# The causal mask of latent attention: a select by index on GpSimd behind the exponential, in place of mask products on TensorE

## The reference

```python
x = x + 0.5 * moe(layernorm(x))            # 8 experts, top 2
x = x + attn(layernorm(x))                 # 16 heads, causal, key offsets by slope
x = x + 0.5 * moe(layernorm(x))
x = x + 0.5 * latent_block(layernorm(x))   # latent attention + small experts
x = x + scan_block(layernorm(x))           # convolution, recurrence, FFN
x = x + 0.5 * latent_block(layernorm(x))
```

```python
att = einsum('bhqd,bhkd->bhqk', q, k) / sqrt(64)
att = where(tril(ones(t, t)), att, -inf)      # key index <= query index
y = einsum('bhqk,bhkd->bhqd', softmax(att), v)
```

## Time and profile before

| | us |
|---|---|
| median of 3 runs | 1462.42 |
| the three runs | 1457.88, 1462.42, 1463.39 |
| the profiled execution | 1457.45 |
| its span, first to last instruction | 1455.6 |
| TensorE busy | 1343.7 |
| VectorE busy | 1006.8 |
| ScalarE busy | 866.9 |
| GpSimd busy | 396.7 |

### The profile page before, as it was taken

The page is one execution under the profiler, slowest core; times in us unless marked ns, Lnnn a source line. Parts: engine busy times, 40 slices in busy tenths (PEclk is TensorE's granted clock), DMA queues, the critical chain, the costliest instruction groups (busy, mean ns, idle before and its releaser), DMA issues.

```text
span 1455.6 us, 27093 instructions
## 1 busy us (share of the span) xinstructions
PE 1343.7 (92%) x10934; PEld 571.7 (39%) x10934; DVE 1006.8 (69%) x1516; ACT 866.9 (60%) x1100; POOL 396.7 (27%) x331
## 2 busy tenths in 40 slices
PE   7899998898889999989999989899988999989997
PEld 5344343333334444433444333443333444433432
DVE  3534778889815457778978757978867687766734
ACT  4344357788773562546567687566765766546672
POOL 5554420011014654522222023021232042202010
PEclk8999999999999999979999999999998999989998
DMA  6623101000005331101111010111010110101100
GB/s 173 118 58 69 33 5 44 3 2 2 2 1 109 121 68 24 26 6 23 34 24 23 1 23 1 34 24 23 1 23 1 23 34 6 26 8 23 24 1 15
DMA packets 30291, 45.80 MB, mean 31 GB/s; under 512 B 5892, under 2 KB 10692, under 8 KB 30116
## 3 DMA queue, kind: packets, MB, share of 16 engines
q1 hardware_dynamic: 30168, 44.08, 13.8%
HBM read 25.39 MB, written 1.18 MB: 18 GB/s over the span
## 4 chain that ended last, share of the span: by engine, by line
PE 76%; ACT 10%; DVE 8%; issue 5%; DMA 0%; POOL 0%; POOLq 0%; ACTq 0%; DVEq 0%; SPq 0%
PE ps L1251 14%; PE ps L1351 12%; PE ps L1296 8%; ACT PR L1429 6%; PE ps L1217 6%; PE ps L1237 5%; PE ps L1218 5%; PE ps L1219 5%; PE ps L1831 3%; DVE BM L1517 2%; PE ps L1315 2%; PE ps L1229 2%; PE ps L1258 2%; PE ps L1362 2%; PE ps L1363 1%
## 5 line engine op out<-in xcount | busy, mean ns | idle before, releaser
L1429 ACT ACTIVATE PR<-ps 128x1024 f32<-128x1024 f32 x432 | 432.4, 1025 | 220.8 <-PE ps L1258 126.2
L1517 DVE TENSOR_REDUCE BM<-ps 128x2 f32<-128x1024 f32 (+2 forms) x384 | 349.6, 951 | 48.0 <-PE ps L1237 47.4
L1251 PE MATMUL ps<-QS,KS 48*128 48x512 f16 (+7 forms) x2688 | 310.5, 333 | 46.6 <-ACT PR L1429 35.0
L1351 PE MATMUL ps<-PR,VS 128*32 128x512 f32 (+3 forms) x2304 | 234.3, 501 | 3.6 <-ACT PR L1429 3.1
L1251 PEld LDWEIGHTS ps<-QS,KS 48*128 48x128 f16 (+1 forms) x2688 | 109.9, 96 | 214.5 <-ACT PR L1429 111.1
L1237 PE MATMUL ps<-KS,QS 48*128 48x128 f16 (+2 forms) x1728 | 161.4, 274 | 15.6 <-DVE BM L1517 6.5
L1510 DVE TENSOR_REDUCE BM<-ps 128x8 f32<-128x1024 f32 x96 | 116.9, 1220 | 35.4 <-PE ps L1237 34.7
L1237 PEld LDWEIGHTS ps<-KS,QS 48*128 48x128 f16 x1728 | 69.0, 95 | 129.2 <-issue 48.0
L1217 PE MATMUL ps<-YA,QS 128*128 128x512 f16 x256 | 99.8, 390 | 1.1 <-DVE RX L1476 1.0
L1558 POOL TENSOR_TENSOR OS<-OS,RX 128x512 f32<-128x512 f32 x24 | 30.5, 1272 | 255.4 <-ACT RX L1445 255.4
L1218 PE MATMUL ps<-YA,QS 128*128 128x512 f16 x256 | 99.3, 388 | 0.0
(11 more groups left out here) (299 smaller groups left out, 2070.3 us busy)
## 6 DMA issues: line engine op xcount, KB each, us to landing
PR<-gates SPq DMA_DIRECT2D x32, 512.0 KB, 11.9
QS<-KS SPq DMA_DIRECT2D x64, 128.0 KB
QS<-KS SPq DMA_DIRECT2D x64, 64.0 KB
WM<-W_in SPq DMA_DIRECT2D x1, 2048.0 KB, 9.1
QS<-HL SPq DMA_DIRECT2D x48, 32.0 KB
KS<-HL SPq DMA_DIRECT2D x48, 32.0 KB
QS<-CT SPq DMA_DIRECT2D x96, 2.0 KB
KS<-KS SPq DMA_DIRECT2D x8, 128.0 KB, 2.4
```

The source lines that it names most:

```text
L1251: ins = pe.matmul(ps[pair][:, w, off:off + cols], KS[rows, ks, kt * P:(kt + 1) * P], QS[rows, qs, (ph + 1) * TT - cols:(ph + 1) * TT], sta ...
L1351: ins = pe.matmul(dst[32 * j:32 * j + 32, TT - cols:TT], v, PR[:, buf, j, off:off + cols], start=(g == 0), stop=(g == NGRP[ph] - 1))
L1429: act.activation(dst, src, ACT.Exp, scale=0.125 if lat else 1.0).then_inc(sig["exp"], 1)
L1517: ins = dve.tensor_reduce(BM[:, ph, p, :, qt - 4 * ph, part], bnk[:, :, off:off + nk * P], AX.X, ALU.max)
```

## The change

For the latent layers alone, the four mask products of each diagonal piece are not issued. The exponential is taken of the unmasked scores. A new GpSimd task `mk` follows the last exponential of each masked group: for every diagonal square of the group one `affine_select` over four heads by 128 queries, in place in `PR`, keeps the element where query index minus key index is not negative and writes 0 elsewhere. `pv` of such a group waits for `mk` in place of the exponential. In the planner the new task costs 0.66 us a square and stands second in GpSimd's order of preference; the masked score steps of the latent plan lose their 0.08 us a piece; and time advances from event to event where it went in steps of 0.02 us, which holds for both plans. The first attention layer keeps its mask products.

```diff
--- before.py
+++ after.py
@@ -155,7 +155,8 @@
                 self.take(s, "pair", x)
                 if i % 2 == 0 and i + 1 < len(SCORES[ph]):
                     continue
-                need = [x]
+                cut = self.LATENT and masked(ph, g)
+                need = [add("POOL", "mk", ("mk", n, ph, g), x) if cut else x]
                 if g == 0:
                     need += values
                 add("PE", "pv", ("pv", n, ph, g), *need)
@@ -209,11 +210,12 @@
         if kind in ("sc", "exp"):
             steps = SCORES[task[2]][task[3]]
             if kind == "sc":
-                return ((0.66 if self.LATENT else 0.23)
-                        + 0.08 * len(steps) * masked(task[2], group_of_step(*task[2:4])))
+                return 0.66 if self.LATENT else 0.23 + 0.08 * len(steps) * masked(task[2], group_of_step(*task[2:4]))
             return 1.03
         if kind == "pv":
             return 0.12 + sum(x[2] for x in group_pieces(*task[2:4])) * 0.0017
+        if kind == "mk":
+            return 0.66 * len(group_pieces(*task[2:4]))
         if kind in ("un", "red"):
             u = UNITS[task[2]][task[3]]
             cols = sum(x[3] for x in u) * P
@@ -331,21 +333,22 @@
         free = {e: 0.0 for e in engines}
         seen, self.start, back = {}, {}, {}
         left = len(self.needs)
+        pending = []
         t = 0.0
         while left:
             for s, own in list(self.held.items()):
-                if all(seen.get(x, 1e9) <= t for x in self.frees[own]):
+                if all(seen.get(x, 1e9) <= t + 1e-9 for x in self.frees[own]):
                     back[s] = max(seen[x] for x in self.frees[own])
                     del self.held[s]
             for e in engines:
-                if free[e] > t:
+                if free[e] > t + 1e-9:
                     continue
                 best = None
                 for s in of[e]:
                     if heads[s] == len(self.streams[s]):
                         continue
                     task = self.streams[s][heads[s]]
-                    if any(seen.get(x, 1e9) > t for x in self.needs[task]):
+                    if any(seen.get(x, 1e9) > t + 1e-9 for x in self.needs[task]):
                         continue
                     room = None
                     if task in self.room:
@@ -380,7 +383,9 @@
                 self.start[task] = t
                 free[e] = t + c
                 seen[task] = t + c + self.LAND.get(task[0], 0.12 if e == "PE" else 0.03)
-            t = round(t + 0.02, 2)
+                pending.append(seen[task])
+            t = min([x for x in list(free.values()) + pending if x > t + 1e-9], default=t + 1)
+            pending = [x for x in pending if x > t]
             assert t < 3000, [self.streams[s][h] for s, h in heads.items() if h < len(self.streams[s])]
         self.seen = seen
         self.count, self.total = {}, {}
@@ -463,7 +468,7 @@
              "DVE": ("ro", "exl", "ewl", "eup", "eh", "ct", "m4", "den", "cen", "scl", "scb", "rt", "gtc", "hf", "gt", "mya", "mup", "cv", "dt0", "dts", "bd",
                      "scn", "st2", "st3", "oup", "fya", "fup", "krot", "krl", "kl", "ksw", "km", "rotd", "rotl", "swp",
                      "bt", "latl", "cp", "add", "red", "gwl", "wql"),
-             "POOL": ("et", "psg", "pct", "pbt", "on", "xl", "ff", "rot", "xql"),
+             "POOL": ("et", "mk", "psg", "pct", "pbt", "on", "xl", "ff", "rot", "xql"),
              "SP": ("gd", "egb", "crow", "put", "kput", "st", "wl1", "wl2")}
 
     def build(self):
@@ -1241,7 +1246,7 @@
 
         def pe_scores(pe, lat, n, ph, i, pair):
 
-            diag = masked(ph, group_of_step(ph, i))
+            diag = masked(ph, group_of_step(ph, i)) and not lat
             for p, kt, off, cols in SCORES[ph][i]:
                 sl, b = slot_of(lat, n) + p, batch_of(n)
                 terms = [(b, sl, 1), (2 + b, sl, 0), (b, sl + 2, 0)] if lat else [(sl, sl, 1)]
@@ -1332,7 +1337,10 @@
                 pe_unit(pe, lat, n, ph, i, slot).then_inc(sig["un"], 1)
             elif kind == "pv":
                 n, ph, g = args
-                pe.wait_ge(sig["exp"], c("exp", n, ph, min(2 * g + 1, LASTS[ph])))
+                if lat and masked(ph, g):
+                    pe.wait_ge(sig["mk"], c("mk", n, ph, g))
+                else:
+                    pe.wait_ge(sig["exp"], c("exp", n, ph, min(2 * g + 1, LASTS[ph])))
                 if g == 0:
                     if not lat:
                         pe.wait_ge(sig["vs"], c("vs", n))
@@ -1550,6 +1558,15 @@
                 pool.wait_ge(s_egb[t % 2][i // 4], egb_value(lat, t))
                 pool.wait_ge(sig["eh"], c("eh", u))
                 pool.tensor_tensor(ring_he(lat, u), ring_he(lat, u), GB[:, t % 2, i // 2, :], ALU.mult).then_inc(sig["et"], 1)
+                return
+            if task[0] == "mk":
+                n, ph, g = task[1:]
+                pool.wait_ge(sig["exp"], c("exp", n, ph, min(2 * g + 1, LASTS[ph])))
+                for _, off, _ in group_pieces(ph, g):
+                    square = PR[:, group(n, ph, g) % NPR, :, off:off + P]
+                    ins = pool.affine_select(out=square, in_=square, compare_op=ALU.is_ge, fill=0.0, base=0,
+                                             pattern=[[0, QUAD], [1, P]], channel_multiplier=-1)
+                ins.then_inc(sig["mk"], 1)
                 return
             n, ph = task[1:]
             pool.wait_ge(sig["rx"], c("rx", n, ph))
```

## The result

The changed kernel takes 1451.26 us, median of 7 runs (1447.14 to 1457.87), against 1459.87 us, median of 7, for the kernel before. The ratio is 0.9948 (0.9932 to 0.9965): faster by 0.5%, some 8 us, in place of the 17 us of the forecast. The profiled execution is the slowest of the seven, with a span of 1456.0 us, which is that of before; its totals can't be compared, its stretches can.

What follows compares the result with a forecast made beforehand. TensorE's issue time was taken as the bound (busy 92% of the span). Terms of -22.3 us for products, +5 for selects and 0 for order gave -17.3 us, from 1462.42 to 1445 us; range 1432 to 1468 us.

Steps and rivals of the forecast that it cites:

- The likeliest case: Whole kernel: 1445 us, own range 1435 to 1454 us, chance 0.52.
- the term for the order: Planner's rewritten order of every stage: centre 0, +-8 us, an eighth of TensorE's 66.8 us idle time after 620 us.
- The term for the products: TensorE, latent layers: dropping 1024 mask products frees 24.3 us of issue time, of which 22.3 us arrive.
- The idle 8%: TensorE's waiting share of the latent stretch, taken to turn part of the 24.3 us saved into waiting, leaving 22.3 us.
- The term for the selects: Latent layers: products with the values wait for GpSimd's selects, adding 5 us, ends 0 and 15 us.
- the overlay in the prediction: Selects and GpSimd rotations laid over 96 masked latent groups' gaps: 15 gaps lengthen by 15.0 us if nothing is moved.
- rival 2: GpSimd's queue: selects behind rotations hold up products, up to 6.9 us a rotation; 1473 to 1488 us, chance 0.12.
- rival 1's bad side: All stages: the planner's new order loses 12 of the 17.3 us gain; 1457 us, chance 0.18.
- the 60 to 80 us: Sign: TensorE's idle time in the latent stretch stays within 60 to 80 us.
- the sign that I had named for rival 3: Latent stretch: TensorE's idle time grows by the 22 us removed and no wait names the select.
- rival 3: TensorE's saved issue time becomes waiting for banks or VectorE's reductions; about 1463 us, chance 0.08.
- more than 3 us would mean that the order counts for itself: Sign: first masked latent exponential starting more than 3 us from 607.32 us means the order counts for itself.

Runs made afterwards that it cites:

- experiment 11: Changed kernel plus a first-layer planner rule: no unit takes the last free single bank while no product with the values holds one; 1446.1 us, ratio 0.99.
- experiment 7: Changed kernel, its orders kept, with neither mask products nor selects in the latent layers; 1451.4 us, ratio 0.994.
- experiment 4: Changed kernel, orders and banks kept, with mask products issued again in the latent layers in place of the selects; 1471.7 us, ratio 1.0085.
- experiment 8: Changed kernel, orders kept, with each select over all columns of its piece in place of the first 128; 1484.8 us, ratio 1.0168.

## Why the prediction was right, and where it was not

The measured 1451.3 us lies in the range, and the sign is right. The likeliest case, 1445 us with its own range of 1435 to 1454, holds it too, but on the slow side, with half of the forecast gain, and by a sum whose terms were off in both directions. That the number fell there is in part luck: the term for the order came to twice its own bound of 8 us, and the two others, 5.1 and 1.7 us better than forecast, took back 6.8 of the 16.

**The term for the products was right.** Forecast -24.3 us, of which 22.3 were to arrive; measured -24.0 us at the order of before, -19.3 and -20.3 us at the two others. The starts in the timeline, 0.09 us for four products, gave this; the 62.4 us of busy time would have promised almost three times as much. The idle 8% took no clear share. A likely reason, not tested by itself, is that the exponentials that TensorE waited for in turn waited for the mask products.

**The term for the selects is right only together with its order.** Forecast +5 us; measured -0.1 us in the order that was planned with them, and 30.9 us in the order of before, where the overlay in the prediction said 15.0 us if nothing moved. The overlay itself was wrong. Done again from the trace of before, with the same allowances and each rotation as the one block that it is, it has the same 13 short gaps and the same nine exponentials that end during a rotation, but six of the nine, not three or four, have their product before the rotation is over, and 17 gaps grow by 29.0 us in all. That is close to the 30.9 us, though each gap is counted by itself, so that two groups behind one rotation count twice. The first pair of the earlier trace rows is one of the six: its exponential ends at 608.36 us, its product starts at 609.93 us, and the rotation runs from 606.12 to 613.34 us. So rival 2 (the queue) is real, as the 5.27 us wait behind a rotation shows, and the changed kernel escapes it only by its order.

**The term for the order is the step that failed.** I put "centre 0, +-8 us". It was +16 us: with no mask, the changed kernel's orders take 1451.4 us where those of before take 1435.2. The profiles of these two kernels, both near their medians, say where. The end of the first quad comes 4.2 us later (about 3 us of that lie before the first exponential of attention, which the same order of the first layer reached at 199.8 us in the profile of the changed kernel and at 202.7 us in this), from there to the router it takes 11.4 us longer, and from the router to the end 1000.4 us against 999.3, 1.1 us more. So, as far as two profiles tell, next to nothing of it lies in the latent layers. The terms -24.0 for the products, +16.2 for the order and -0.1 for the selects add up to -7.9 us, and the medians say -8.6 us; since each is the difference of neighbouring kernels on one path from the one to the other, they must add up, and this is no test. On another path, with the selects put in before the order is changed, they are -24.0, +30.9 and -14.8 us. On both, selects and order together cost 16 us, where the sum had 5. The mechanism is rival 1's bad side, which I gave 0.18 and priced at 12 us. The bound that I took, an eighth of TensorE's idle time, had no ground in a row, and it was taken for the latent stretch, while the loss came in the first layer.

Why the order is worse is shown for the first layer. In the plan the score steps and units may hold all four pairs of banks. When the ring is full, the scores wait for the exponentials, those for the product with the values, and that product for a single bank; each pair that VectorE frees goes to the next unit at that very moment. As I read it, with steps of 0.02 us the product found a moment between, and with exact events it did not until the units had run as far ahead as they may. The first layer's plan has this gap in its own times (12.6 us between two exponentials; with the old steps its longest is 6.6 us, at another place), the chip has it at 12.1 us, and the rule of experiment 11 removes both. The stall at 1181 us has the same form, and it is there with the selects left out (11.5 us in experiment 7); that the same rule would cure it was not tried, since it rewrites every latent order. Whether making room for the selects by itself costs the latent plan anything stays open: the 10.2 and 18.0 us under the table point that way both times, but the chance of an order and the room for the selects can't be told apart there.

Of the signs named: 512 products left, none after 600 us, right; 128 selects of about 0.65 us, 0.675; GpSimd 266.8 us after 620 us for 254, as the later start moved work behind 620 us; TensorE idle 83.8 us there, over the 60 to 80 us. That is 17 us more than before, close to the sign that I had named for rival 3; experiment 4 rules rival 3 out by the time itself. The exponential that ends the first masked latent group started at 620.3 us, 13 us late, and the prediction had said that more than 3 us would mean that the order counts for itself. It did. The 0.77 us a select that I had estimated from the Trainium skill, GPSIMD Engine Reference, section Performance versus the Vector engine, was too much: 675 ns is the measurement. VectorE's scaling, which once took 2652 ns, at 608.71 us in the middle of that rotation, did not stretch further: its longest is 1372 ns here. VectorE is busy 1014.6 us with the selects and 1011.9 us without them at the same order (experiment 7), so they cost it 3 us at the most that these two profiles show.

## What to carry to other kernels

Where a planner writes the order, a change of its clock, a cost or a tie-break is a change to every stage, and here it was worth 10 to 20 us either way in a stage, as much as the work that was removed. Measure a mechanism at a fixed order (swap the instructions, keep the lists), and the order with the mechanism left out. Work moved to an idle engine can be free where the order was made with its latency in it, and dear elsewhere: the same selects cost 0, 18 and 31 us in three orders. But that order has its own price, so compare also with the best order without the work. When you lay new work over a queue, count a job of several instructions as one block. And in a plan, look for resources that one kind of task can take the moment they are freed: the longest gap between two exponentials in the first layer's plan would have shown this stall before any run.

## What the runs showed of the hardware that was not expected

A select on GpSimd takes about half of the two-input product on the same engine (675 ns for 512 fp32 elements a partition against 1.29 us), and it grows by 0.80 ns an element: (1953 - 727) / 1536 from experiment 8. And the clock granted to TensorE fell to 1.2 GHz without a long wait before it. In the latent stretch it was still 1.00 at 1185 us and 0.50 from 1186 us on (0.96 and 0.50 in the two windows), after TensorE had issued from 1181.17 us on a unit every 1.13 us, with waits of 0.74 us at the most between them; at 270.5 us the waits before the fall were 0.80 us at the most. I had looked for such a fall only behind long waits.
